# Order of instructions in a three-stage decoder kernel: four places of an iteration, the banks of x2's halves, and the last two batches

## The reference, cut to what matters

```python
x = layernorm(x + attention(x))        # 16 heads of 32, causal, Wq Wk Wv Wo with biases
x = layernorm(x + wkv(decay, first, k=x, v=ctx))   # recurrence over the 256 tokens, per channel
x = layernorm(x + moe_attention(x))    # below

gating = softmax(x @ W_gate.T)         # 16 heads; the best one per token
q, k, v = split(x @ W_qkv.T)
k_shared = k of the token's best head; v_shared = v of that head * its gate value
y = causal attention of all 16 query heads over the one shared key and value
```

## Time and profile before

| | us |
|---|---|
| median of 3 runs | 1510.12 (1509.27 to 1512.72) |
| profiled execution | 1509.66 |
| its span, first to last instruction | 1507.8 |

### The profile page before, as it was taken

The page is one execution under the profiler, slowest core; times in us unless marked ns, Lnnn a source line. Parts: engine busy times, 40 slices in busy tenths (PEclk is TensorE's granted clock), DMA queues, the critical chain, the costliest instruction groups (busy, mean ns, idle before and its releaser), DMA issues.

```text
span 1507.8 us, 26652 instructions
## 1 busy us (share of the span) xinstructions
PE 1397.5 (93%) x9908; PEld 1112.9 (74%) x9908; DVE 1095.7 (73%) x2258; ACT 650.5 (43%) x1459; POOL 378.6 (25%) x520
## 2 busy tenths in 40 slices
PE   7887899999999999999999999999999999998796
PEld 6676778777777877777777777777777777876563
DVE  4464777777777777777777778777787776779753
ACT  3453435345353534535354453525444352544223
POOL 1244312222131222213122221312232232222200
PEclk9999999999999999999999999999999999999997
DMA  6531323324142332314333241333313233330210
GB/s 184 154 92 36 92 78 82 96 56 103 35 104 81 83 95 54 103 37 99 85 82 96 52 101 41 92 92 82 96 40 98 56 92 92 82 82 18 55 44 29
DMA packets 63199, 119.50 MB, mean 79 GB/s; under 512 B 14304, under 2 KB 32736, under 8 KB 63072
## 3 DMA queue, kind: packets, MB, share of 16 engines
q1 hardware_dynamic: 60128, 112.03, 29.4%
q10 hardware_dynamic: 2944, 5.77, 1.1%
HBM read 32.81 MB, written 8.39 MB: 27 GB/s over the span
## 4 chain that ended last, share of the span: by engine, by line
PE 63%; DVE 19%; issue 3%; SPq 2%; ACT 2%; DMA 1%; POOL 0%; ACTq 0%; POOLq 0%; DVEq 0%
PE po L591 7%; PE pp L486 6%; PE pp L488 6%; PE pp L487 6%; DVE neg_max L1527 5%; PE pw L486 4%; PE pw L488 4%; PE pw L487 4%; PE sk L564 3%; PE sq L532 3%; PE sk L511 3%; PE po L595 3%; PE po L605 3%; PE sq L511 3%; PE sq L526 2%
## 5 line engine op out<-in xcount | busy, mean ns | idle before, releaser
L1527 DVE TENSOR_REDUCE neg_max<-sq 128x2 f32<-128x512 f32 (+1 forms) x384 | 252.7, 686 | 126.7 <-PE sq L511 125.1
L1161 ACT ACTIVATE prob<-sk 128x512 f32<-128x512 f32 x384 | 215.9, 597 | 250.7 <-PE sk L511 248.0
L486 PE MATMUL pp<-xt_hi,w_hi 128*128 128x256 f32 x616 | 189.1, 307 | 18.7 <-DVE w_lo L1514 7.6
L488 PE MATMUL pp<-xt_hi,w_lo 128*128 128x256 f32 x616 | 175.8, 285 | 0.0
L487 PE MATMUL pp<-xt_lo,w_hi 128*128 128x256 f32 x616 | 175.7, 285 | 0.0
L1172 ACT ACTIVATE o_ch<-po 128x512 f32<-128x512 f32 x128 | 76.2, 595 | 167.0 <-PE po L595 167.0
L486 PEld LDWEIGHTS pp<-xt_hi,w_hi 128*128 128x128 f32 x616 | 120.0, 195 | 23.2 <-issue 19.4
L2048 POOL TENSOR_TENSOR w_ev<-w_e,w_val 128x256 f32<-128x256 f32 x64 | 45.8, 716 | 360.0 <-ACT w_e L1218 319.3
L511 PE MATMUL sk<-mask_kq,ident_b 128*128 128x256 bf16 (+1 forms) x384 | 124.4, 324 | 0.0
L511 PE MATMUL sq<-mask_qk,ident_b 128*128 128x256 bf16 (+1 forms) x384 | 124.4, 324 | 0.0
L487 PEld LDWEIGHTS pp<-xt_lo,w_hi 128*128 128x128 f32 x616 | 119.6, 194 | 0.3
(11 more groups left out here) (203 smaller groups left out, 3679.6 us busy)
## 6 DMA issues: line engine op xcount, KB each, us to landing
q_stack<-q_hi SPq DMA_DIRECT2D x256, 128.0 KB, 2.4
q_stack<-q_lo SPq DMA_DIRECT2D x128, 128.0 KB, 2.4
k_stack<-k_hi SPq DMA_DIRECT2D x128, 128.0 KB, 2.3
x_raw<-in_xT SPq DMA_DIRECT2D x16, 512.0 KB, 3.9
k_stack<-k_lo SPq DMA_DIRECT2D x64, 128.0 KB, 2.3
x<-in_x SPq DMA_DIRECT2D x16, 512.0 KB, 4.4
w_val<-in_ctxT SPq DMA_DIRECT2D x64, 128.0 KB, 2.2
out_y<-x SPq DMA_DIRECT2D x13, 512.0 KB, 2.8
```

The costliest lines, as they stand in the source:

```text
L486: T.matmul(out, lh, rh, start=(c == 0), stop=False, skip_group_check=True)
L488: mm = T.matmul(out, ll, rh, start=False, stop=(c == CC - 1), skip_group_check=True)
L1161: A.activation(dst, sk[n % 2][:], ACT.Exp, scale=SCALE).then_inc(s_exp, 1)
L1527: V.tensor_reduce(dst, src, AX.X, ALU.max, negate=True).then_inc(s_max, 1)
```

## The change

The diff is given whole but for context lines. In TensorE's list x2's first half goes to bank pp and its second to pw, and the projection of the queries waits for the second half's lo part only before its third chunk. ScalarE's and VectorE's functions follow with the banks. In an iteration ScalarE's out_hi(t, 1) stands one call earlier, VectorE's out_lo(t, 0) stands ahead of divide(r, 2), and maxima_f(b, 1, 0, 1) stands ahead of pick_value(chf, b, 1). In `ending` second_residual(LAST, 0) stands ahead of pick_key(chn, n, 0), second_norm(LAST) ahead of pick_value(chn, n, 1), and the third stage's statistics and norm of batch 13 stand later on VectorE, ScalarE and GpSimd.

```diff
@@ TensorE @@
             def x2_transpose(b):
                 pe.wait_ge(x2_ready, b + 1)
+                pe.wait_ge(pa_free, values_done(min(b + 2, NB)))
+                wait(pe, pf_free, PF_JOBS * b)
+                turn_half(pp, x_of(b), 0).then_inc(pf_job, 1)
...
-                turn_half(pw, x_of(b), 0).then_inc(u_job, 1)
-
-                pe.wait_ge(pa_free, values_done(min(b + 2, NB)))
-                wait(pe, pf_free, PF_JOBS * b)
-                turn_half(pp, x_of(b), 1).then_inc(pf_job, 1)
+                turn_half(pw, x_of(b), 1).then_inc(u_job, 1)
...
             def project_f(b, job, middle=None):
+                each = None
                 if job == PF_Q:
-                    pe.wait_ge(u_free, U_JOBS * b + U_X2 + 1)
+                    def each(c):
+                        if c == HC:
+                            pe.wait_ge(u_free, U_JOBS * b + U_X2 + 1)
...
-                    mm = channels_out(bank, W_FQ, job - PF_Q, middle)
+                    mm = channels_out(bank, W_FQ, job - PF_Q, middle, each=each)
@@ ScalarE, iteration @@
                 exps_a(t, 2, 0, 1)
+                out_hi(t, 1)
                 exps_a(t, 2, 2)
-                out_hi(t, 1)
                 row_hi_a(t, 3)
@@ ScalarE @@
             def x2_split_hi(b):
-                for half, s_job, count, bank in ((0, u_job, U_JOBS * b + U_X2 + 1, pw),
-                                                 (1, pf_job, PF_JOBS * b + PF_X2 + 1, pp)):
+                for half, s_job, count, bank in ((0, pf_job, PF_JOBS * b + PF_X2 + 1, pp),
+                                                 (1, u_job, U_JOBS * b + U_X2 + 1, pw)):
@@ ScalarE, ending @@
                 row_hi_f(n, 0, f_mrow[NG - 1], 32 * n)
+                x2_split_hi(LAST)
+                exps_f(n, 0, 0, 1)
+                for stk in f_stk:
+                    act.wait_ge(stk, 48 * LAST)
+                fq_hi(LAST, 0)
+                row_hi_f(n, 1)
+                exps_f(n, 0, 2)
+                copy_f(n, 0)
                 third_norm(b, x_of(b))
                 store_whole(b)
                 b = LAST
-                x2_split_hi(b)
-                exps_f(n, 0, 0, 1)
-                for stk in f_stk:
-                    act.wait_ge(stk, 48 * b)
-                fq_hi(b, 0)
-                row_hi_f(n, 1)
-                exps_f(n, 0, 2)
-                copy_f(n, 0)
@@ VectorE @@
-                bank, s_free = ((pw, u_free), (pp, pf_free))[half]
+                bank, s_free = ((pp, pf_free), (pw, u_free))[half]
@@ VectorE, iteration @@
                 sums(r, 3)
+                out_lo(t, 0)
                 divide(r, 2)
-                out_lo(t, 0)
...
                     rows_f(b, 0)
+                    maxima_f(b, 1, 0, 1)
                     pick_value(chf, b, 1)
                     assert chf.n == F_LINK_PICKED + 1
-                    maxima_f(b, 1, 0, 1)
@@ VectorE, ending @@
                 sums(LAST, 3)
+                second_residual(LAST, 0, x_of(LAST))
                 pick_key(chn, n, 0)
-                second_residual(LAST, 0, x_of(LAST))
...
                 key_copy(n)
-                third_stats(b, x_of(b))
                 gate_value(chn, n)
...
                 maxima_f(n, 0, 2)
+                second_norm(LAST, x_of(LAST))
                 pick_value(chn, n, 1)
-                second_norm(LAST, x_of(LAST))
                 rows_f(n, 0)
                 maxima_f(n, 1, 0, 1)
+                x2_split_lo(LAST, 0)
+                x2_split_lo(LAST, 1)
+                maxima_f(n, 1, 2)
+                third_stats(b, x_of(b))
                 b = LAST
-                x2_split_lo(b, 0)
-                x2_split_lo(b, 1)
-                maxima_f(n, 1, 2)
@@ GpSimd, ending @@
+                inverse_std(LAST, 1)
                 inverse_std(b, 2)
                 third_bias(b)
-                inverse_std(LAST, 1)
```

## The result

The changed kernel takes 1456.38 us (median of 4 runs, 1454.89 to 1457.90) where the kernel before took 1509.69 beside it (4 runs, 1508.84 to 1512.72): a ratio of 0.9643, 95% interval 0.9627 to 0.9660. Forecast were 1458.1 us and a range of 1452 to 1476. The profiled execution took 1456.15 us, with a span of 1454.3.

A forecast was written before the change was run, and what follows sets the result against it. TensorE, plus the few places where it stands still, was taken to bound the loop. Gains of 46.3 us (t = 2 to 15), 2.4 (t = 1) and 2.9 (last two batches) made 51.6 off 1509.66: 1458.1 us, range 1452 to 1476.

The forecast's parts named there:

- The restart: TensorE's waits behind a 512-column matmul: each costs its idle time plus 0.16 us, since the next matmul would start earlier.
- Edit 1: Loop, x2: halves exchange banks and projection Q waits for the second only at c = 2, gaining 0.66 us an iteration.
- Edit 2: Loop, VectorE: out_lo(t, 0) ahead of divide(r, 2) removes the maxima transpose's wait for k_lo, gaining 1.4 us an iteration.
- Edit 3: Loop, ScalarE: out_hi(t, 1) ahead of group 2's last exps removes a 0.29 us k_lo wait, gaining 0.45 us an iteration.
- Edit 4: Loop, VectorE: maxima_f(b, 1, 0, 1) ahead of pick_value(b, 1) gains 0.98 us, less 0.16 at the third maximum: 0.82.
- t = 1 and the first edits of t = 2: Start of the loop: in t = 1 shorter k_lo waits, 1.65 and some 0.8 us, were to give 2.4 us.
- The last two batches: Kernel's end: reordered residual, statistics and norm, with upstream gains, move the start of batch 15's Q 2.9 us earlier; bounds 1 and 6.
- Rival B: Last batches, 1422 to 1430 us: the half-clock stretch goes, giving about 3 us more, so 1455 us; chance 0.15.
- Rival A: Loop: the maxima's second DMA becomes late; a 3.3 us round trip loses 19.6 us in all, so 1478; chance 0.15.
- Rival C: Loop, VectorE: k_lo late by 0.7 us and the third maximum by 0.4, costing 15.4 us, so 1474; chance 0.1.
- D: Loop: the maxima's DMA round trip exceeds 6.0 us, making the kernel slower; at 7 us, 1525 us; chance 0.03.
- E: Loop: no effect, since the moved waits are held by another engine anyway; 1509.7 us; chance 0.03.

The follow-up runs named there:

- maxf: The kernel before with only maxima_f(b, 1, 0, 1) moved ahead of pick_value(b, 1): 13.2 us less in whole time, 1.07 us an iteration.
- ending: The kernel before with only the changes of the last two batches, none of the loop's four: 2.4 us less.
- loop: The kernel before with the loop's four changes and none of the last two batches': 47.8 us less.
- statsback: The changed kernel with third_stats of batch 13 back in its old place ahead of gate_value on VectorE: 2.7 us more by the ratios.

## Why the prediction was right

In the loop its mechanism held, and the sum was 1.7 us off (1458.1 for 1456.38). That it came so near is partly luck. Between the profiled executions 53.5 us were gained for 51.6 forecast, and in this the four edits gave 3.8 us more than their terms, the clock in the last batches gave 2.1 that no term had, DMA waits took 2.6 that no term had, and the part ahead of the first key transpose gave 1.6 less. Step by step:

- **The restart, idle time plus 0.16 us.** Right on average. Idle times of 0.41, 1.38, 0.29 and 0.82 us gave 0.66, 1.46, 0.46 and 1.07, when taken away one at a time; with the idle time alone the four would come to 2.9 us, and 3.65 were measured. The surplus was 0.25, 0.08, 0.17 and 0.25 us: a mean of 0.19, and no constant.
- **Edit 1, 0.66.** Measured 0.66, and by its two undoings 0.6. That it takes both the exchange and the split wait is shown.
- **Edit 2, 1.4.** Measured 1.46. The forecast left 0.1 for a k_lo that comes late, and it didn't.
- **Edit 3, 0.45.** Measured 0.46.
- **Edit 4, 0.82.** Measured 1.07; here the give-back of 0.16 at the third maximum did not come. In the changed kernel it ends 0.06 us before its transpose starts. I had left VectorE's chain from the first pick to the third maximum as long as it was, 7.15 us; it ran in 6.90, one short instruction taking 0.24 for 0.48 (L1708, the product behind the second pick's sum). That is no scatter: it took 0.47 to 0.49 us there in every one of t = 2 to 14 before, and 0.24 in all of maxf and of the changed kernel. So a length read in one order did not hold in the other, by more than the 0.16 that I built on it; why it is shorter there, no run tells. The remaining 0.1 above 0.98 isn't explained either.
- **The sum, 14 x 3.33 = 46.6.** Per iteration 3.6 measured. From the first to the last of 14 key transposes it would be 13 x 3.6 = 46.8, and is 44.2: the two DMA waits grew. Iterations over the undisturbed distance cost 4.2 us in all before and 6.8 after. This loss was in no term; the overshoot of edit 4 covered it.
- **t = 1 and the first edits of t = 2.** 2.4 and 2.5 were forecast. Kernels that are the same up to there differ by 3 us (197.4 and 200.8 us from the first matmul to the first key transpose in before and ending; 194.3, 195.0 and 191.8 in after, loop and statsback). The means differ by 5.4, which agrees, but one trace couldn't have shown it.
- **The last two batches, 2.9.** 6.0 measured in the three stretches, of which about 0.8 is edit 4 in iteration 15, counted with the 14. Their sum was right. From iteration 15's key transpose to the start of Q of batch 15 it was 1425.28 - 1353.80 = 71.48 us and is 1373.92 - 1306.34 = 67.58: 3.9 less, or 3.1 without edit 4, for 2.9 forecast. The 1.47 of third_stats was 1.46, the wait for GpSimd's root 0.52 where 0.6 was put, and ending shows 0.6 for the 0.65 of third_residual in its first stretch. Edit 1's two terms came out smaller: taking back either half of it costs 0.1 us in the first stretch and 0.6 between batch 14's key transpose and Q, where 0.5 and 0.85 were put. The other 2.1 us lie behind Q, for which the sum had no term. From there to the end TensorE is busy 2.4 us less for the same 393 matmuls, at a granted clock of 0.88 for 0.85 (19.0 us at the half clock for 24.5); first before, then after:

```profile
1425.30:1507.80 82.50, 63.85 (x393) 45.68 (x393) 36.96 (x86) 24.80 (x49) 2.47 (x8) 0.85 0.12 33
```
```profile
1373.90:1454.30 80.40, 61.46 (x393) 43.93 (x393) 39.03 (x92) 25.91 (x51) 3.73 (x12) 0.88 0.15 41
```

  Rival B had foreseen such a gain, with 3 us and a chance of 0.15, for the one stretch of the earlier trace rows; here it came in part and spread over the end.
- **What is late next.** Rival A did not come from the round trip: the slack was 0.89 us, not 0.3. The 2.35 us of the earlier trace rows came from iteration 14 of the kernel before, one of its three slow ones, so I bounded a steady path by a disturbed row. Rival C's late k_lo and third maximum did not occur, and D and E were far off.

The two DMA waits that did come up have another cause than A had: an issue of SyncE's that starts together with a 16 KB instruction block of TensorE's can take 1.4 to 2.1 us. Shifting the blocks moved the long issue and took the wait for the k stacks away. That it is the packet itself that holds the issue, and by what path, was not separated: the 64 instructions shifted all 80 at once.

## What to carry to other kernels

Waits of the bound engine that repeat with the same idle time in each iteration can be priced one by one, idle time plus the restart, and added, as long as the other engines wait for the bound engine somewhere between them (a loop without such waits was not tried here). Bound the next-late path with rows of undisturbed iterations. Where a tail doesn't profit from gains ahead of it, compare TensorE's idle time and its busy time in it one by one: here the idle time had fallen and the half clock had made the same matmuls longer. And when a pattern has been mended in the loop, look for its copy in the written-out ending (here worth 3.3 us, 1.3 and 2.0, ahead of Q of batch 15).

## What the runs showed of the hardware

- SyncE's DMA issues become long beside TensorE's instruction blocks. In the changed kernel every one of SyncE's issues above 1.4 us from 333 us on starts within 0.2 us of a packet of the instruction queue, and 15 of the 18 issues above 0.9 us between 150 and 1340 us overlap one. Most blocks do no harm: of the 69 in that time 47 overlap an issue, and 15 of these a long one; 17 begin inside an issue of the row maxima (4 KB), and none of those issues took over 0.7 us. With 64 instructions more on TensorE the long issues were others; no row of a wait names this.
- A 4 KB transfer on chip took 1.80 us from the start of its issue to the matmul that waited for it, and each issue held SyncE for 0.62 to 0.68 us.
- A reordering upstream shifts where the half clock falls. In loop it put 6.8 us of it into a stretch where before and the changed kernel have none, and the stretch behind the last key transpose, nearly the same work in all fourteen kernels of the table, took 45.9 to 48.5 us. A gain under 2 us in the tail can't be read from the whole time.
- One short VectorE instruction (128x32 by a scalar) took 0.48 us where it stood ahead of the maxima, in t = 2 to 14 of the kernel before, and 0.24 where it stood ahead of a residual, in all of the changed kernel.
